# Two more waits of GpSimd in each group of the second edge stage: the rows of all gathers but the latest must have landed

## The reference, cut to what matters

```python
h = jax.nn.silu(edge_scalars @ fc_w1 * (1.0 / math.sqrt(NES))) * SILU_NORM
w = h @ fc_w2 * (1.0 / math.sqrt(FCN))              # 256 weights for each edge
...
xg0 = y0[edge_src]                                  # 64 columns of the source node's row
xg1 = y1[edge_src]                                  # 192 columns of it
...
mids = jnp.concatenate([mid0, mid1, mid2.reshape(-1, 3 * MUL), mid3.reshape(-1, 3 * MUL)], axis=1)
agg = jax.ops.segment_sum(mids, edge_dst, num_segments=n)
```

## Time and profile before

| | |
|---|---|
| runs of the kernel | 4357.1, 4372.39, 4376.29 us (median 4372.39) |
| the profiled execution | 4357.34 us, its span 4355.6 us |
| mean granted clock of TensorE | 0.833 |
| TensorE busy | 3384.6 us (78% of the span) |
| VectorE busy | 2266.0 us (52%) |
| GpSimd busy | 1898.9 us (44%) |
| ScalarE busy | 1433.0 us (33%) |
| gathers of the second edge stage | 834, from 2104.0 to 3933.3 us, 949 ns each in the median |
| DMA traffic | 375.93 MB, mean 86 GB/s |

### The profile page before, as it was taken

How to read it: one execution, slowest core, us unless ns; L and a number is a source line. 1 busy time by engine, 2 the same in 40 slices (tenths; PEclk the granted TensorE clock), 3 DMA queues, 4 the chain that set the end, 5 groups by cost and what they waited for, 6 DMA issues and landing times. The chain is left out here.

```text
span 4355.6 us, 80354 instructions
## 1 busy us (share of the span) xinstructions
PE 3384.6 (78%) x22728; PEld 2463.9 (57%) x22728; DVE 2266.0 (52%) x6165; ACT 1433.0 (33%) x4367; POOL 1898.9 (44%) x2266
## 2 busy tenths in 40 slices
PE   6577777766777787999588888778887777878679
PEld 4466666655666665888344444444444444446568
DVE  5455555555555575766344444444444444456732
ACT  5122222222222173333133333333333333314612
POOL 3655656666556310111444444444444444451144
PEclk9678888888888898999678778887777877879889
DMA  6333333333333464322322222222222222223511
GB/s 196 109 88 84 86 85 91 87 85 87 84 87 93 105 191 127 92 85 75 91 66 67 64 65 67 68 67 64 65 65 66 66 64 66 67 80 97 172 42 48
DMA packets 239107, 375.93 MB, mean 86 GB/s; under 512 B 88190, under 2 KB 145606, under 8 KB 238762
## 3 DMA queue, kind: packets, MB, share of 16 engines
q0 software_dynamic: 89712, 230.26, 19.2%
q1 hardware_dynamic: 147482, 140.83, 11.6%
q10 hardware_dynamic: 1696, 2.62, 0.2%
HBM read 310.75 MB, written 62.84 MB: 86 GB/s over the span
## 5 line engine op out<-in xcount | busy, mean ns | idle before, releaser
L1980 POOL DMA_INDIRECT e_rows<-tab,e_ix x828 | 788.4, 952 | 1006.6 <-DVE e_msg L2154 679.5
L586 POOL DMA_INDIRECT e_rows<-tab,e_ix x830 | 794.0, 957 | 533.5 <-issue 254.2
L2222 PE MATMUL e_pU<-e_msg,e_oh 128*32 128x128 f32 (+1 forms) x6672 | 557.8, 337 | 312.2 <-issue 307.3
L2152 DVE TENSOR_TENSOR e_msg<-e_pW,e_rows 128x256 f32<-128x256 f32 x417 | 176.8, 424 | 925.3 <-remote 680.6
L2222 PEld LDWEIGHTS e_pU<-e_msg,e_oh 128*32 128x32 f32 x6672 | 297.7, 120 | 553.5 <-issue 495.0
L981 PE MATMUL e_pU<-e_ohp,e_rows 128*128 128x128 f32 x3340 | 531.8, 321 | 89.8 <-issue 85.9
L981 PEld LDWEIGHTS e_pU<-e_ohp,e_rows 128*128 128x128 f32 x3340 | 503.3, 235 | 103.6 <-issue 96.9
L2208 PE MATMUL e_pW<-e_w,e_hT 64*128 64x256 f32 x1668 | 396.8, 513 | 51.2 <-DVE e_msg L2154 22.4
L2154 DVE TENSOR_TENSOR e_msg<-e_pW,e_rows 128x384 f32<-128x384 f32 x834 | 422.2, 548 | 0.0
L695 ACT CAST e_ohT<-e_pT 64x640 bf16<-64x640 f32 x167 | 114.6, 686 | 900.0 <-remote 511.6
L2038 ACT COPY e_us<-e_pU 96x512 f32<-96x512 f32 x139 | 80.9, 582 | 752.4 <-PE e_pU L2222 653.3
(11 more groups left out here) (453 smaller groups left out, 5713.5 us busy)
## 6 DMA issues: line engine op xcount, KB each, us to landing
e_rows<-tab,e_ix POOLq DMA_INDIRECT x1658
xnT<-f_xnT SPq DMA_DIRECT2D x25, 250.0 KB, 3.2
e_xk<-xnT SPq DMA_DIRECT2D x25, 250.0 KB
xnT<-b_xT SPq DMA_DIRECT2D x25, 250.0 KB, 3.0
m_xnT<-xnT SPq DMA_DIRECT2D x25, 250.0 KB
xnT<-m_xT SPq DMA_DIRECT2D x25, 250.0 KB, 2.7
ffn_norm<-xnT SPq DMA_DIRECT2D x25, 250.0 KB
tab<-f_hrow SPq DMA_DIRECT2D x25, 227.5 KB
```

What stands on the lines that cost most here:

```text
L586: nc.gpsimd.indirect_dma_start(out=rows[:, s, j, :], out_offset=None, in_=env["tab0"], in_offset=bass.IndirectOffsetOnAxis(ap=at[:, j:j + ...
L1980: nc.gpsimd.indirect_dma_start(out=rows[:, r % PER, j, :], out_offset=None, in_=env["tab1"], in_offset=bass.IndirectOffsetOnAxis(ap=at[:, ...
L2222: last = nc.tensor.matmul(u8[:, 0:8:2, :] if c == 0 else u8[:, 1:2 + 2 * c:2 * c, :], oh[:, r % 2, ST * i + j, c, :], m[:, 0:4, :] if c == ...
```

## The change

Four lines are added in GpSimd's loop over the tiles of a group, in the second edge stage alone. At the fourth tile (j == 3) GpSimd also holds until gather 1 of the same group has landed; at the first tile (j == 0), from the second group on, until gather 4 of the group before has landed. Each is two instructions, a wait and the empty instruction behind it.

```diff
--- before.py
+++ after.py
@@ -1974,6 +1974,10 @@
                             if lo >= 1:
                                 for i in ((j,) if j < 3 else range(3, T1) if j == 3 else ()):
                                     hold(pool, s_row[i], 16 * g)
+                            if j == 3:
+                                hold(pool, s_row[1], 16 * (g + 1))
+                            elif j == 0 and lo >= 1:
+                                hold(pool, s_row[T1 - 2], 16 * g)
                             if j == 3 and hi <= GROUPS1 - 2:
                                 nc.gpsimd.tensor_copy(ix[:, (r + 1) % 2, :], srcI[:, bass.ds((g + 1) * T1, T1)])\
                                   .then_inc(s_ix, 1)
```

## The result

The changed kernel takes **3892.25 us** (median of 4 runs, 3882.36 to 3908.33) against 4367.62 us: a ratio of 0.8916, 95% interval 0.8879 to 0.8954, so 11% faster. The forecast was 4115 us with a range from 3980.

The account below looks back on a forecast made before the run. It took TensorE to be starved while gathers follow closely in the second edge stage. From 4357 us it took 213 (groups), 20 (clock) and 15 (start), added 5 (group 0's wait): 4114, so 4115 us, range 3980 to 4440.

Parts of the forecast that it names:

- What bounds the kernel: Second edge stage: TensorE starved while gathers follow closely, recovering in pauses; it stands 307.3 us before the window sums.
- At the first tile: Wait for the previous group's fifth gather: costs nothing, as GpSimd stands some 6 us there anyway, except in the first groups.
- The pause at the fourth tile: Idle time between third and fourth gather grows from 0.37 to 1.15 us, bounds 0.37 and 1.6 us.
- What a pause returns: The fourth-tile pause returns 12 matmuls a group to TensorE before it starves, bounds 0 and 26.
- the same slope: 74 matmuls per us of pause beyond TensorE's release, from first-edge-stage rows where 0.19 us gave 14.
- The group: Second edge stage: a group falls from 13.51 to 11.8 us, 1.6 us less with rounding, 213 us over 133 groups.
- GpSimd's cover: Added 0.8 us a group on GpSimd is hidden by 6.2 us of idling, gone only below 9.2 us a group.
- The clock term: With fewer stalls TensorE's granted clock gains 0.15 us a group, 20 us in all, bounds 0 and 140.
- The start: First groups of the second edge stage: 15 us returned from the freeze, 5 us lost by group 0's fourth gather waiting.
- the freeze: VectorE's 33.19 us stand at the stage's start, while GpSimd issues 36 gathers in a row; about half would return.
- The rule against it: DMA engines alternate queue rows packet by packet, so no backlog counts; splitting a burst would return nothing, time as no change.
- no change: Rival, chance 0.12, 4357 us: second gather already landed at the wait, or the burst's later end takes the pause's return.

Follow-up runs that it names:

- c4_pause10: Changed kernel with both waits replaced by ten GpSimd filler copies at each place, chip 4 (with the stall): 3863.8 us, ratio 0.8957 to the kernel before.
- c1_after: The changed kernel itself, run again on chip 4 (with the stall): 3860.3 us, ratio 0.8945 to the kernel before.
- e1_fourth_only: Changed kernel without the wait at the first tile, only that at the fourth kept, chip 13: 4091.6 us, ratio 0.9373 to the kernel before.
- c3_pause6: Changed kernel with both waits replaced by six copies at each place, the fourth tile's index copy counted, chip 4: 4114.9 us, ratio 0.9538 to the kernel before.
- e4_drained: Changed kernel with each wait asking for the latest gather's rows too (third and sixth), chip 13: 4227.6 us, ratio 0.9664 to the kernel before.
- d3_after: The changed kernel itself, run on chip 3 (without the stall): 3551.4 us against 3343.6, ratio 1.0620 to the kernel before.

## Why the prediction was wrong

- **What bounds the kernel: right.** TensorE was starved while gathers follow each other closely, and pauses of GpSimd are the cure; a pause made of copies does the same as the wait (c4_pause10 and c1_after).
- **At the first tile: "nothing, except in the first groups". This step failed, and it is the largest.** GpSimd stood 6 us there because the message was late, and the message was late because of the stall. With the stall small the message is early, the wait binds (1.33 us in the median), and without it the burst of six only moves across the border of two groups. The forecast priced one wait: e1_fourth_only, which has only that one, took 4091.6 us, against 4115. That the two are near is luck: the pause was longer and returned more than forecast (next two points), and the bursts that cross the border took it back. The other wait is worth the remaining 190 to 200 us.
- **The pause at the fourth tile: 1.15 us, measured 1.45.** The copy's 0.19 us and the 0.49 us from it to the gather stood in the sum as 0.1 us, 0.6 us too little; landing and waking were 0.3 us quicker than the 2.3 us taken (in the median the copy starts 2.02 us after the second gather's end).
- **What a pause returns: too little.** I had 12 matmuls for 1.15 us and, at the same slope, none for 0.95 us. c3_pause6, with 0.96 us, came to 11.75 us a group, the value that the forecast gave to 1.15 us (11.8). Then 1.46 us returned so much that GpSimd's own pace, 9.88 us, set the group (c4_pause10). The bound of 26 matmuls for up to 1.6 us was too low.
- **The group: 11.8 us, measured 9.87.** So 3.6 us less than 13.51, not 1.6, and 459 us over the stage, not 213.
- **GpSimd's cover: the sum was right, its use wrong.** "Gone only below 9.2 us a group" is 9.7 us with the true pauses, and I took it to be far off. It is where the kernel now stands. e4_drained gave the rule: 4230 us expected from GpSimd's sum, 4227.6 measured.
- **Clock and start.** The clock term was 20 us with a bound of 140. The clock of the stage rose from 0.79 to 0.90, the value of d3_after too, and TensorE's busy time fell by 310 us for the same records; no run tells the clock's share of this from that of sums stretched by the stall, nor what of it lay on the path. The start was to gain 10 us and lost 1.4 (up to the eighth group). The fourth gather of group 0 did wait 4.29 us, as forecast; the freeze went, but GpSimd's six groups ahead now take longer.
- **The rule against it.** The forecast gave 0.12 to "no change", 4357 us, and the time was 3892.25: splitting the burst did return something. The Trainium skill (DMA: Bandwidth & Descriptors, Queues, rings and completion order) says that a DMA engine takes turns between its queue rows packet by packet. What failed is the step from there to "returns nothing", since no record shows that TensorE lacks something that a DMA engine brings; the page's rule itself is not tested by any run here.

Not settled is what TensorE lacks in the stall, and why chip 3 does not have it. The profiles before, after and of d3_after move the same 375.93 MB in the same queues, and between 2856 and 2859.9, where TensorE waits in the earlier trace rows, the only records are those of the gathers' own queue.

## What to carry to other kernels

When a stall makes an engine wait somewhere, that wait is no cover for a cost put there: with the stall gone it is gone, so price a new wait in the kernel as it will be, by the pace of the engine that gets it (here that of GpSimd, 5.7 + 1.2 + two pauses: 4227.6 us for 4230 expected in e4_drained, 3551.4 for 3556 in d3_after). Judge a change that works around starvation on more than one chip: this one brought 11% in both comparisons on chips with the stall and costs 6% on the one without. A pause that is only a pause need be no longer than it must; before the kernel is given waits on a landing, the length that suffices should be measured with filler.

## What the runs showed that I had not expected

- The same kernel takes 4312 to 4378 us on three chips and 3344 us on a fourth, each within 0.5% over its runs. What differs in the traces is that TensorE is late under gathers on the three (some 310 us of "issue" and 680 us of VectorE's wait in the second edge stage of the kernel before) and not in any kernel on the fourth, at the same gather durations (949 and 946 ns) and the same landing times. The kernel before has no profile on chip 3, so that this makes up the whole 1000 us is not shown.
- With two pauses of 1.46 us a group takes what GpSimd alone needs (9.88 us in c4_pause10), though TensorE is still late in it; with copies for 0.96 us at both places it takes 2.9 us more than that (11.75 against 8.86). Only with pauses of 2.56 and 2.74 us is TensorE hardly late any more (e4_drained), and GpSimd's group is then 12.4 us long.
- A GpSimd copy of 128x6 words between two gathers adds only 0.08 us to their distance, since it lies in a gap that is there anyway; each further one adds 0.12 us.
